# Attention kernel, two layers: a scaled key group and an output scaling placed ahead of PSUM copies, one repeat of sums given from VectorE to ScalarE

## The reference

```python
def _gqa_forward(hidden_state, encoder_hidden_state, mask, ...):      # layer 0: 32 heads of 16, 8 key heads
    q, k, v = hidden_state @ Wq + bq, encoder_hidden_state @ Wk + bk, encoder_hidden_state @ Wv + bv
    ...
    attn = jax.nn.softmax(scores + mask, axis=-1)
    x = attn_out @ Wo + bo + hidden_state
    return (x - mu) * jax.lax.rsqrt(var + EPS) * gamma + beta
...                                                                   # layer 1: 16 heads of 32
a = _layer_norm(audio_kv, ln_gamma, ln_beta)
Q, K, V = hidden_states @ Wq.T, a @ Wk.T, a @ Wv.T
attn = jax.nn.softmax(jnp.where(mask, scores, -inf), axis=-1)
return hidden_states + jnp.tanh(gate) * (attn_out @ Wo.T)
```

## Time and the profile before

| | us |
|---|---|
| median of 3 runs | 1171.71 (1170.9 to 1172.59) |
| the profiled execution | 1169.72 |
| its span in the trace | 1167.9 |
| PE busy | 1119.5 |
| DVE busy | 822.0 |
| ACT busy | 757.9 |
| POOL busy | 246.7 |

### The profile page before, as it was taken

How to read it: one execution, slowest core, us unless ns; L and a number is a source line. 1 busy time by engine, 2 the same in 40 slices (tenths; PEclk the granted TensorE clock), 3 DMA queues, 4 the chain that set the end, 5 groups by cost and what they waited for, 6 DMA issues and landing times.

```text
span 1167.9 us, 28618 instructions
## 1 busy us (share of the span) xinstructions
PE 1119.5 (96%) x10003; PEld 952.6 (82%) x10003; DVE 822.0 (70%) x2626; ACT 757.9 (65%) x2307; POOL 246.7 (21%) x264
## 2 busy tenths in 40 slices
PE   3999999999999999999999999999999999999998
PEld 3678788887888888788787878888788888878886
DVE  4465777768588686858768686876868678686845
ACT  3464857748485784848668484866848486584844
POOL 2041212122131212213121221312122131112210
PEclk9799999999999999999999999999999999999999
DMA  7665546647464664646456454745735474574320
GB/s 238 186 181 118 143 105 145 157 94 177 102 166 105 134 167 94 164 107 156 125 119 170 104 147 115 162 118 120 179 93 156 108 169 117 118 185 94 105 65 8
DMA packets 78077, 155.23 MB, mean 133 GB/s; under 512 B 10528, under 2 KB 47200, under 8 KB 77296
## 3 DMA queue, kind: packets, MB, share of 16 engines
q1 hardware_dynamic: 77936, 153.40, 53.6%
HBM read 113.72 MB, written 39.65 MB: 131 GB/s over the span
## 4 chain that ended last, share of the span: by engine, by line
PE 75%; ACT 8%; DVE 7%; issue 7%; DMA 2%; SPq 1%; POOL 1%; DVEq 0%; ACTq 0%; POOLq 0%
PE PJ L358 19%; PE TP L409 8%; PE SCO L395 6%; ACT PR L1045 6%; PE OA L429 5%; PE PJ L461 5%; PE SCO L677 5%; PE SCO L409 5%; PE SCO L453 5%; PE PJ L371 4%; PE SCO L358 3%; PE OA L434 2%; DVE PR L813 2%; PE SCO L399 1%; ACT PT L1056 1%
## 5 line engine op out<-in xcount | busy, mean ns | idle before, releaser
L1045 ACT ACTIVATE PR<-PR,MN 100x361 f32<-100x361 f32 x768 | 451.8, 591 | 101.1 <-DVE MN L813 97.9
L813 DVE CUSTOM_DVE_ANT_0 PR<-SCO,MK 100x361 f32<-100x361 f32 x768 | 384.7, 530 | 120.5 <-PE SCO L395 80.2
L409 PE MATMUL TP<-ident,PR 100*128 100x100 f32 x1536 | 195.5, 249 | 1.9 <-ACT PT L1056 1.9
L409 PEld LDWEIGHTS TP<-ident,PR 100*128 100x128 f32 x1536 | 167.2, 141 | 26.2 <-ACT PR L1045 2.1
L395 PE MATMUL SCO<-K0S,Q0S 128*100 128x362 f32 x512 | 151.2, 367 | 3.2 <-DMA K0S<-k_scr 1.3
L1045 ACT ACTIVATION_READ_ACCUMULATOR PR<-PR,MN 100x1 f32 x768 | 145.8, 190 | 0.0
L825 DVE COPY PT<-TP 121x300 f32<-121x300 f32 x256 | 119.5, 467 | 14.8 <-PE TP L409 13.6
L1056 ACT ACTIVATE PT<-TP 121x300 f32<-121x300 f32 x256 | 103.4, 404 | 24.7 <-PE TP L409 24.7
L409 PE MATMUL SCO<-ident,PR 100*128 100x100 f32 x768 | 110.0, 252 | 4.4 <-ACT PT L1056 4.4
L1217 POOL TENSOR_TENSOR K1F<-K1F,KB 128x364 f32<-128x364 f32 x64 | 50.8, 793 | 263.9 <-DVE K1F L806 263.9
L409 PEld LDWEIGHTS SCO<-ident,PR 100*128 100x128 f32 x768 | 84.3, 141 | 22.1 <-issue 7.7
(11 more groups left out here) (144 smaller groups left out, 2052.5 us busy)
## 6 DMA issues: line engine op xcount, KB each, us to landing
K1S<-k_scr SPq DMA_DIRECT2D x128, 364.0 KB, 6.2
k_scr<-K1HL SPq DMA_DIRECT2D x64, 364.0 KB, 2.7
Q0S<-q_scr SPq DMA_DIRECT2D x128, 100.0 KB, 4.2
K0S<-k_scr SPq DMA_DIRECT2D x64, 182.0 KB, 4.9
AT<-ctx_cols SPq DMA_DIRECT2D x16, 722.0 KB, 9.7
V<-ctx_rows SPq DMA_DIRECT2D x16, 484.0 KB
q_scr<-QHL SPq DMA_DIRECT2D x16, 400.0 KB, 2.5
k_scr<-K1HL SPq DMA_DIRECT2D x32, 182.0 KB, 3.2
```

The lines of the kernel that those rows point to most:

```text
L409: last = pe.transpose(turned(k)[:, c * T:(c + 1) * T], PR[0:T, k % NPR, c * SP:c * SP + P], ident[0:T, 0:T])
L813: dve.tensor_tensor_reduce(out=PR[0:T, k % NPR, 0:S], in0=SCO[0:T, k % 2, 0:S], in1=mask[0:T, :], scale=scale, scalar=3.4e38, op0=ALU.add, ...
L1045: act.activation(PR[0:T, k % NPR, 0:S], PR[0:T, k % NPR, 0:S], ACT.Exp, bias=MN[0:T, k:k + 1], scale=-1.0, accum_out=SM[0:T, k:k + 1]).the ...
```

## The change

Four edits, all in the order or the place of work that exists already:

- VectorE, step 0 of each batch but the first: `keys1_scaled` of group 2 stands ahead of the copy of pair 21 (was behind it).
- VectorE and ScalarE, step 5 of each batch but the first: `unit_outputs` stands ahead of VectorE's copy of pair 2, and `unit_sums` ahead of the exponentials of heads 8 and 9.
- ScalarE, step 23: the copy of pair 20 stands ahead of both exponentials (was between them).
- All batches: the repeat of unit 1's reciprocals (L836) is made by ScalarE, between its third copy of layer-1 values and its copy of pair 15. VectorE keeps the reciprocals.

```diff
@@ VectorE
                 dve.reciprocal(RSM[0:T, :], SM[0:T, 16 * u:16 * u + 16]).then_inc(rcp, 1)
+                if u == 1:
+                    return
                 wait_from(dve, attn, 3 * b + u)
...
+                    if not first and p == 0:
+                        keys1_scaled(b, 2)
+                    elif not first and p == 5:
+                        unit_outputs(b - 1, 2)
                     if p >= 3:
                         probs_out(b, p - 3)
                     elif not first:
                         probs_out(b - 1, NPAIR - 3 + p)
-                    if not first and p == 0:
-                        keys1_scaled(b, 2)
-                    elif not first and p == 3:
+                    if not first and p == 3:
                         keys1_scaled(b, 3)
...
-                    if p == 5 and not first:
-                        unit_outputs(b - 1, 2)
@@ ScalarE
+            def repeat_sums(b):
+                act.wait_ge(attn, 3 * b + 1)
+                act.wait_ge(rcp, 3 * b + 2)
+                src = RSM[0:T, :].rearrange("p (a g j) -> p g j a", a=2, g=2).unsqueeze(4).to_broadcast([T, 2, NJ, 2, HD0])
+                act.activation(SX[0:T, 0:2, :].rearrange("p g (j a d) -> p g j a d", j=NJ, a=2), src, ACT.Copy)\
+                    .then_inc(sums_x, 1)
...
+                    if p == 5 and not first:
+                        unit_sums(b - 1, 2, C * T)
                     if p > 0:
                         exps(b, 2 * p - 2)
                         exps(b, 2 * p - 1)
...
-                    if p == 5 and not first:
-                        unit_sums(b - 1, 2, C * T)
...
                 probs_out(b, 14)
                 values1(b, 2, PJ[0:SP, 0, :])
+                repeat_sums(b)
                 probs_out(b, 15)
...
-                    if p == 19:
+                    if p in (19, 23):
                         probs_out(b, p - 3)
                     exps(b, 2 * p - 2)
-                    if p > 19:
+                    if 19 < p < 23:
                         probs_out(b, p - 3)
                     exps(b, 2 * p - 1)
```

## The result

| | before, us | changed, us |
|---|---|---|
| median, runs | 1172.63, 6 | 1166.25, 6 |
| lowest to highest | 1170.9 to 1173.92 | 1165.33 to 1168.32 |
| the profiled execution | 1169.72 | 1168.32 |
| its span | 1167.9 | 1166.5 |

The ratio is 0.995, with a 95% interval of 0.9936 to 0.9963: 5.9 us faster, 4.3 to 7.5.

The account below looks back on a forecast made before the run. The prediction took TensorE, busy 96% of the span, as the bound, so only its waits could be won. Terms 0.3 + 5.7 + 0 + 1.4 = 7.4 us, from 1171.71 to 1164.3 us; range 1160 to 1169.8.

Parts of the forecast that it names:

- The scaling ahead of the copy of pair 21: VectorE, step 0: value product starts 0.38 us sooner, mostly lost before the last `out_half`; 0.3 us, bounds 0 and 5.7.
- The rival of the whole 0.38 us: Last `out_half` does not wait for the copy of pair 23, so the scaling's whole gain counts; 1158.9 us, chance 10%.
- The outputs ahead: Step 5, ahead of VectorE's copy of pair 2: `out1` starts 0.38 us sooner in 15 batches; 5.7 us, bounds 0 and 6.0.
- The cover for ScalarE's copy of pair 2: Step 5: this copy, delayed 0.29 us to end at 550.16, still precedes TensorE's need at 550.38; covered by 0.2 us.
- The copy of pair 20: ScalarE, step 23: moving it ahead of an exponential releases nothing; 0 us, bounds 0 and 1.6 us.
- The repeat on ScalarE: Unit 1's repeat costs ScalarE 334 to 490 ns in idle time; VectorE's hold delays `keys0` less; 1.4 us gain.
- the upper bound of 3.9 us for every wait gone: Upper bound of the ScalarE repeat's gain: every wait for the split context gone, 2.5 + 1.4 us.
- GpSimd doesn't follow: GpSimd's start hangs on DMAs that may not move with TensorE; up to 5.3 us given back, 1169.6 us, chance 13%.
- The hold only moves: End of GpSimd's work alone sets `keys0`, so the ScalarE repeat's 1.4 us fall away; 1165.7 us, chance 9%.

Follow-up runs that it names:

- e2: Kernel before with only key group 2's scaling moved ahead of VectorE's copy of pair 21: ratio 0.9997 to the kernel before.
- e5: Changed kernel with VectorE's reciprocals and repeat of unit 2 moved from step 1 to step 2, behind the copy of pair 23: ratio 0.997 to the kernel before.
- e6: Kernel before with unit 2's reciprocals and repeat moved behind the copy of pair 23, without the scaling ahead: ratio 1.0039, 4.6 us slower.
- e1: Kernel before with only unit 2's outputs and sums moved ahead: ratio 0.9947, 6.2 us faster.
- e4: Kernel before with only ScalarE's copy of pair 20 moved ahead of both exponentials: ratio 0.999.
- e3: Kernel before with only unit 1's repeat moved to ScalarE: ratio 0.9993, 0.8 us faster.
- e8: Kernel before with SyncE issuing query columns, output and residual rows ahead of the load of key groups 2 and 3: ratio 0.9973, 3.2 us faster.
- e7: Changed kernel with SyncE issuing query columns, output and residual rows ahead of the load of key groups 2 and 3: ratio 0.9917 to the kernel before.
- e12: e7 with unit 2's repeat behind the copy of pair 23 and group 3's scaling ahead of the copy of pair 0: ratio 0.9898 to the kernel before.
- e9: e7 with unit 2's outputs on VectorE at the head of step 5, ahead of both heads: ratio 0.9882 to the kernel before.

## Why the prediction was right, and what stays open

The forecast was 1164.3 us from a gain of 7.4 us; measured are 1166.25 us and a gain of 5.9, 4.3 to 7.5, inside the range of 1160 to 1169.8. The time is 0.25 us above the band that the forecast gave itself (1162.5 to 1166); 0.9 of the 1.95 us by which it misses is the kernel before, whose median rose from 1171.71 to 1172.63 us with three more runs.

- *The scaling ahead of the copy of pair 21: 0.3 us forecast.* Alone it gives 0.9997 (e2), and both profiles show the 0.38 us won at the value product and gone at `out_half`. That VectorE's unbroken run up to the copy of pair 23 holds it there was argued and is now shown: with the repeat out of the run and the scaling ahead `out_half` starts 0.38 us sooner (e5), with the repeat out alone it doesn't move (e6). The prediction named the copy itself. The experiments moved the copy and the masks of heads 4 and 5 ahead of it together, so they don't tell them apart; the traces do in part. The recorded wait is that of head 7's scores for the mask of head 5, which the prediction did not have, and head 6's scores did start 0.37 us sooner, which it said they would not. But the weights of `out_half` are loaded 0.11 to 0.12 us after the copy's end in every profile, whether head 7's scores ended at 5.82 us (before) or at 5.75 (changed). Both belong to the same run, which is why the price was right. (The run holds one scaling and not two, as the prediction lists it.) The rival of the whole 0.38 us is out.
- *The outputs ahead: 5.7 us forecast.* Alone 6.2 us, 4.3 to 8.2 (e1). In the traces `out1` starts 0.38 us sooner in the batch, and the first head of layer 1 starts at 54.67 us, in before at 55.15. Nothing gave the 0.38 us back. The cover for ScalarE's copy of pair 2 sufficed.
- *The copy of pair 20: 0 forecast.* 0.999, with 1 inside its interval (e4).
- *The repeat on ScalarE: 1.4 us forecast.* Its cost was right: 416 ns, between the bounds of 334 and 490, in idle time; the estimate of 0.51 us beside them was too high. Its mechanism was right: 1.76 us after GpSimd's share and no longer 2.33 (e3). Its size is open: alone it measured 0.8 us, from 2.3 faster to 0.7 slower. I priced it from the landing times of one execution, and whether a batch waits at all differs by more than this term: the same changed kernel waited 4.2 us and 1.8 us in two profiles. It was also counted in the wrong place: of the 0.55, 0.49 and 0.37 us by which `keys0` was late in batches 5, 4 and 13 of before, only 0.43, 0.38 and 0.24 are left at layer 1's first head (55.29, 55.24 and 55.10 us into the batch, against 54.86), 1.05 us instead of 1.4. And the upper bound of 3.9 us for every wait gone was too low: e8, in which none is left, took 4.5 us less over batches 1 to 14. It is the weakest term of the sum, and the measured total, 1.5 us below the forecast, leaves room for it to be anything down to nothing; that it is what the forecast has too much was not shown, since the interval reaches to 7.5 us.
- *GpSimd doesn't follow.* The prediction named a sign for it, `keys0` idle for more than 2.5 us in total, and the sign came: 4.2 us in the first profile. It was a bad sign, since in the second it was 1.8. Read by its start instead, the rival is out: its start moved by 0.56 us in e1, by 0.25 and 0.45 in the two profiles of the changed kernel, against four profiles without the outputs' edit that lie between 34.72 and 34.79 (before, e2, e3, e4). `keys0` starts at 39.77 us on the mean in before and at 39.42 and 39.26 in the changed kernel, 0.35 and 0.51 sooner, about the 0.38 of `out1`.
- *The hold only moves*: as a time, 1165.7 us, it can't be told from the forecast, and the 1166.25 measured lie nearer to it; as a mechanism it is half true. The context's copy is held in place of the repeat, 2.79 us at 507.49, and what queues behind the hold is one copy less. The port rule of the Trainium skill (SBUF — State Buffer, Who interferes with whom) says that one of the two engines has the shared pair for a whole instruction while the other is blocked; the trace agrees, and here the block lasted over the rest of one GpSimd instruction (507.09 to 508.36) and the whole of the next (to 510.07). That the lateness of the rows is what counts was shown by e7 and e8, which end the wait with the repeat on either engine.

## What to carry to other kernels

A wait that TensorE shows is worth what the next wait behind it leaves over. Before pricing a reorder, follow the engine that does the moved work from there on: if it runs without a gap to the next thing that is waited for, the gain is nothing until that run is shortened, and what is pushed out of the run must not land ahead of the following one (e5, e6, e12). Where an engine idles ahead of a piece, put the needed work into that gap and not only ahead of a copy (e9). Price a delay at the next thing that all of the work behind it hangs on: part of what was lost at `keys0` was made up before layer 1 began. And where a wait comes and goes from batch to batch, look for the DMA at its root: one exchange in SyncE's order gave 3.2 us alone (e8) and some 3.9 us on top of the change (e7), against 5.9 us for the change.

## What the runs showed beyond that

- Batch 0 took 86.5 to 86.8, 88.1 to 88.5 or 90.1 us in the profiles, with a granted clock of 0.86, 0.72 or 0.57 to 0.60 between 42 and 54 us, in kernels whose code of batch 0 is nearly the same. In this stretch TensorE runs for part of the time at the lower of its two levels, 1.2 GHz, and for the rest at 2.4 GHz, in a different share from execution to execution. The step of 1.7 us is larger than several of the effects studied here, so profiles were compared from batch 1 on.
- A VectorE copy from SBUF to SBUF of 0.34 us took up to 2.79 us while GpSimd worked, and a copy from PSUM at 507.10, beside GpSimd's work from 507.09, 0.47 us as ever. The repeat of unit 1, from SBUF to SBUF too, took VectorE 0.29 to 3.06 us in before and ScalarE 415 to 417 ns in all sixteen batches.
